# Second attention's planes reloaded one by one, the third plane copied on the chip, keys and the first quarter of queries ahead of the rest

## The reference, cut to what matters

```python
# layer 0: wavelet bands of x; ll is [8,128,32,32], N = 1024
q, k, v = conv1x1(ll, qkv_w)                 # 8 heads of 16 channels
attn = clip(l2norm(q) @ l2norm(k).T * 16**-0.5)
attn = softmax(keep the 512 largest of each row)
ll_out = group_norm(conv1x1(attn @ v, proj_w))
high_out = high + alpha * gn(conv1x1(silu(gn(dwconv3x3(high)))))
out = x + 0.1 * iwt(ll + ll_out, high_out)
out = out + 0.1 * gn(conv1x1(gelu(gn(conv1x1(out, w1))), w2))
# layer 1: one head of 16 channels over n = 4096 pixels
q, k, v = Wq x + bq, Wk x + bk, Wv x + bv
attn = softmax(q.T k / 4)                    # [4096, 4096]
x = gamma * (Wo (v attn.T) + bo) + x
```

## Time and profile before

| what | value |
|---|---|
| median of three runs | 5599.7 us |
| the profiled execution's own time | 5598.09 us |
| its span | 5596.3 us |
| PE, PE weight load, DVE, ACT, POOL busy | 85%, 55%, 83%, 76%, 5% |
| line 565 (PE): busy, idle just before it | 848.3 us, 115.2 us |
| line 1940 (DVE): busy, idle just before it | 1396.5 us, 291.9 us |
| mean granted clock of TensorE | 0.916 of full speed |

### The profile page before, as it was taken

How to read it: one execution, slowest core, us unless ns; L and a number is a source line. 1 busy time by engine, 2 the same in 40 slices (tenths; PEclk the granted TensorE clock), 3 DMA queues, 4 the chain that set the end, 5 groups by cost and what they waited for, 6 DMA issues and landing times.

```text
span 5596.3 us, 93339 instructions
## 1 busy us (share of the span) xinstructions
PE 4769.4 (85%) x30180; PEld 3089.7 (55%) x30180; DVE 4622.6 (83%) x9087; ACT 4266.1 (76%) x6779; POOL 261.7 (5%) x125
## 2 busy tenths in 40 slices
PE   4444899988999889988999889998899979997799
PEld 2001366654666446663666546664566636664588
DVE  4888799987999789987999879997899979996553
ACT  3884799948998589966999489985899669995333
POOL 2001000020000200010000200002000100000000
PEclk7555899998999989998999989999899989999899
DMA  1001200012001110012000120011200120001100
GB/s 57 7 11 51 63 15 16 15 57 66 16 20 49 38 48 18 16 61 63 15 16 14 58 66 16 20 44 37 54 16 18 60 64 15 16 13 44 36 12 16
DMA packets 101990, 187.43 MB, mean 33 GB/s; under 512 B 47640, under 2 KB 52664, under 8 KB 95832
## 3 DMA queue, kind: packets, MB, share of 16 engines
q1 hardware_dynamic: 101464, 181.02, 11.2%
HBM read 110.09 MB, written 69.47 MB: 32 GB/s over the span
## 4 chain that ended last, share of the span: by engine, by line
DVE 37%; PE 32%; issue 16%; ACT 7%; DMA 3%; SPq 2%; DVEq 1%; POOL 1%; ACTq 0%; POOLq 0%
PE PS L599 11%; DVE M L1772 8%; DVE MX L1940 8%; PE PS L565 5%; DVE work L1763 5%; PE PS L541 3%; ACT work L1194 3%; DVE work L1755 3%; DVE arena L1869 3%; PE PS L583 3%; PE PS L531 2%; PE PS L463 2%; ACT work L1247 1%; PE PS L1068 1%; PE PS L978 1%
## 5 line engine op out<-in xcount | busy, mean ns | idle before, releaser
L599 PEld LDWEIGHTS PS<-V,work 128*128 128x128 f32 x16384 | 2102.7, 192 | 163.4 <-ACT work L1255 23.0
L599 PE MATMUL PS<-V,work 128*128 128x129 f32 x16384 | 2122.1, 276 | 13.6 <-ACT work L1255 12.3
L1194 ACT ACTIVATE work<-arena,T 128x1024 bf16<-128x1024 f32 x1504 | 1715.5, 1144 | 63.0 <-DVE T L1713 47.8
L1940 DVE TENSOR_REDUCE MX<-PS 128x1 f32<-128x512 f32 x2048 | 1396.5, 686 | 291.9 <-PE PS L565 276.5
L1255 ACT ACTIVATE work<-PS 128x1024 f32<-128x1024 f32 x1024 | 1042.2, 1019 | 314.0 <-PE PS L583 312.1
L565 PE MATMUL PS<-KP,QP 96*128 96x512 bf16 x2048 | 848.3, 416 | 115.2 <-DMA QP<-scr 57.6
L1772 DVE MAX8 M<-work 128x8 f32<-128x512 f32 x1024 | 651.8, 681 | 0.5
L1186 ACT ACTIVATE arena<-PS 128x1024 f32<-128x1024 f32 x512 | 524.3, 1024 | 151.8 <-PE PS L463 142.6
L583 PE MATMUL PS<-QP,KP 99*128 99x512 bf16 x2048 | 620.5, 385 | 22.7 <-ACT work L1255 19.4
L1869 DVE SCALAR_TENSOR_TENSOR arena<-PS,work 128x512 f32<-128x512 f32 x896 | 601.3, 684 | 28.7 <-ACT work L1247 18.4
L1247 ACT ACTIVATE work<-PS 128x512 f32<-128x512 f32 x896 | 514.8, 592 | 112.9 <-PE PS L531 109.6
(11 more groups left out here) (193 smaller groups left out, 4158.2 us busy)
## 6 DMA issues: line engine op xcount, KB each, us to landing
work<-scr SPq DMA_DIRECT2D x752, 32.0 KB, 1.8
work<-in_x SPq DMA_DIRECT2D x16, 1024.0 KB, 6.7
arena<-in_x SPq DMA_DIRECT2D x8, 2048.0 KB, 10.8
scrX<-arena SPq DMA_DIRECT2D x8, 2048.0 KB, 6.7
XR<-scrX SPq DMA_DIRECT2D x64, 256.0 KB, 2.7
out<-YO SPq DMA_DIRECT2D x64, 256.0 KB, 2.1
scr<-work SPq DMA_DIRECT2D x24, 512.0 KB, 2.6
scrL<-work SPq DMA_DIRECT2D x24, 512.0 KB, 8.0
```

The lines of the kernel that those rows point to most:

```text
L599: last = mm(PS[:, 5 + i // 2, 136 * (i % 2):136 * (i % 2) + 129], P1[:, (16 * j + k) % 3, t, 128 * i:128 * i + 128], V1[:, mt, :], start=( ...
L1194: A(junk[:, m % 2, :], scores(h, i), ACT.Sign, scale=-1.0, bias=T[:, h % 2, i:i + 1], accum_out=CA[:, h % 2, i:i + 1]).then_inc(s["ca"], 1)
L1940: V.reduce_max(MX[:, c % 2, i, w:w + 1], PS[:, maxbank(c, k, l0), :], AX.X).then_inc(s["mr"], 1)
```

## The change

Three things change, all of them in DMAs, on SP's list.

First, the operands of the second attention. Plane 2 is no longer stored and reloaded: each 16-row block of plane 2 is copied from PT1 to its place by four copies of 16 rows by 2 KB (32 KB), one for each quarter of the pixels. Planes 0 and 1 are still stored by four DMAs each, but the loads of a plane wait for that plane alone (scrw1 for plane 0, scry1 for plane 1). The keys come first, over all pixels (three loads of plane 0, two of plane 1), then the first quarter of the queries (five loads of 32 KB), then, behind a wait for p12, the four key copies and one query copy of plane 2. These fifteen raise qp1, and the first maximum waits for them alone. The other three quarters of the queries follow (five loads of 96 KB, three copies of 32 KB) and raise a new semaphore qp2, for which the first maximum of chunk 2 waits.

Second, head 0 of the next image. The store of plane 0 is followed by its six loads, then come the stores of planes 1 and 2, the two on-chip copies of plane 2, and the four loads of plane 1, each group behind a semaphore of its own (scrw, scrv, scru).

Third, three guards on ACT: before its first eviction of head 1 (which writes over PT1) it also waits for qp1 and qp2, and before the first exponential of a chunk 0 (which writes over PT) for scru.

```diff
@@ -281,15 +281,26 @@
                         if t in parts:
                             sp.dma_start(QK0[HD * j:HD * j + HD, h % 3, w, :], scr0[t, d, w, :]).then_inc(done, 16)
 
-            def load_planes(parts):
-                for w, dst in ((1, KP1), (0, QP1)):
-                    for j, pair in enumerate(TERMS):
-                        if pair[w] in parts:
-                            sp.dma_start(dst[HD * j:HD * j + HD], scr1[pair[w], HD * w:HD * w + HD, :]).then_inc(s["qp1"], 16)
-
-            def store_plane(n, t, made):
+            def store_plane1(f, t, made, done):
+                sp.wait_ge(s[made], f + 1)
+                for j in range(4):
+                    sp.dma_start(scr1[t][:, N0 * j:N0 * j + N0], PT1[32 * j:32 * j + 32, t, :]).then_inc(s[done], 16)
+
+            def load_plane1(w, dst, t, cols, done):
+                for j, pair in enumerate(TERMS):
+                    if pair[w] == t:
+                        sp.dma_start(dst[HD * j:HD * j + HD, cols], scr1[t, HD * w:HD * w + HD, cols]).then_inc(s[done], 16)
+
+            def copy_plane1(w, dst, t, parts, done):
+                for j, pair in enumerate(TERMS):
+                    if pair[w] == t:
+                        for i in parts:
+                            sp.dma_start(dst[HD * j:HD * j + HD, N0 * i:N0 * i + N0],
+                                         PT1[32 * i + HD * w:32 * i + HD * w + HD, t, :]).then_inc(s[done], 16)
+
+            def store_plane(n, t, made, done):
                 sp.wait_ge(s[made], (n + 1) * 2)
-                sp.dma_start(scr0[t].rearrange("p w n -> p (w n)"), PT[:, t, :]).then_inc(s["scrw"], 16)
+                sp.dma_start(scr0[t].rearrange("p w n -> p (w n)"), PT[:, t, :]).then_inc(s[done], 16)
 
             def head0_late():
                 for j, pair in enumerate(TERMS):
@@ -404,25 +415,34 @@
                 if fin:
                     load_done(f, False)
                 if opn:
-                    store_plane(n, 0, "p0")
-                    store_plane(n, 1, "p1")
+                    store_plane(n, 0, "p0", "scrw")
                     sp.wait_ge(s["vt"], (n + 1) * 2)
                     sp.sem_inc(s["free"], 1)
-                    sp.wait_ge(s["scrw"], n * 48 + 32)
-                    load_head(0, (0, 1))
-                    store_plane(n, 2, "p2")
+                    sp.wait_ge(s["scrw"], (n + 1) * 16)
+                    load_head(0, (0,))
+                    store_plane(n, 1, "p1", "scrv")
+                    store_plane(n, 2, "p2", "scru")
                     head0_late()
+                    sp.wait_ge(s["scrv"], (n + 1) * 16)
+                    load_head(0, (1,))
                 if fin:
-                    for a, made in enumerate(("p10", "p11", "p12")):
-                        sp.wait_ge(s[made], f + 1)
-                        for j in range(4):
-                            sp.dma_start(scr1[a][:, N0 * j:N0 * j + N0], PT1[32 * j:32 * j + 32, a, :])                                .then_inc(s["scrw1" if a < 2 else "scry1"], 16)
-                    sp.wait_ge(s["scrw1"], (f + 1) * 128)
-                    load_planes((0, 1))
+                    store_plane1(f, 0, "p10", "scrw1")
+                    store_plane1(f, 1, "p11", "scry1")
+                    first, rest = slice(0, N0), slice(N0, N1)
+                    sp.wait_ge(s["scrw1"], (f + 1) * 64)
+                    load_plane1(1, KP1, 0, slice(0, N1), "qp1")
                     sp.wait_ge(s["scry1"], (f + 1) * 64)
-                    load_planes((2,))
+                    load_plane1(1, KP1, 1, slice(0, N1), "qp1")
+                    load_plane1(0, QP1, 0, first, "qp1")
+                    load_plane1(0, QP1, 1, first, "qp1")
+                    sp.wait_ge(s["p12"], f + 1)
+                    copy_plane1(1, KP1, 2, range(4), "qp1")
+                    copy_plane1(0, QP1, 2, range(1), "qp1")
+                    load_plane1(0, QP1, 0, rest, "qp2")
+                    load_plane1(0, QP1, 1, rest, "qp2")
+                    copy_plane1(0, QP1, 2, range(1, 4), "qp2")
                 if opn:
-                    sp.wait_ge(s["scrw"], (n + 1) * 48)
+                    sp.wait_ge(s["scru"], (n + 1) * 16)
                     for h in range(1, 3):
                         load_head(h)
                 if fin:
@@ -555,8 +575,10 @@
                     if c == 0 and k == 1 and l0:
                         pe.wait_ge(s["de"], (b + 1) * 6)
                     if k == 0 and c == 0:
-                        pe.wait_ge(s["qp1"], b * 192)
+                        pe.wait_ge(s["qp1"], b * 240)
                         pe.wait_ge(s["v1c"], b * 8)
+                    if k == 0 and c == 2:
+                        pe.wait_ge(s["qp2"], b * 128)
                     if k == 0 and c >= 2:
                         pe.wait_ge(s["y1"], a * NCH + c + (1 if l0 else 0))
                     elif k == 0 and c == 1:
@@ -1209,8 +1231,10 @@
                     if h >= 2:
                         act.wait_ge(s["pv"], (b * NH + h - 2) * NT + i + 1)
                     if h == 1 and i == 0:
-                        need(act, s["scrw1"], b * 128)
+                        need(act, s["scrw1"], b * 64)
                         need(act, s["scry1"], b * 64)
+                        need(act, s["qp1"], b * 240)
+                        need(act, s["qp2"], b * 128)
                         need(act, s["xs"], b * 16)
                     act.wait_ge(s["S"], (b * NH + h) * NT + i + 1)
                     stored(h, i)
@@ -1251,6 +1275,8 @@
                         return
                     act.wait_ge(s["st1"], a * 128 + j * 16 + k + 1)
                     act.wait_ge(s["pv1"], a * 128 + j * 16 + (k + 1 if j or k else 3))
+                    if l0 and j == 0 and k == 0:
+                        need(act, s["scru"], (b + 1) * 16)
                     u = pairbanks(k, l0)
                     A(P1[:, (16 * j + k) % 3, :, :].rearrange("p t n -> p (t n)"), PS[:, u:u + 2, :].rearrange("p a n -> p (a n)"),
                       ACT.Exp, scale=0.25).then_inc(s["e1"], 1)
```

More of the change, by code:

```diff
@@ L257, in dwt_attention_kernel @@
           st e p pv o od rd odr ol oc pj fnd fsum dll cv pw x1 dgl f1 hc ge f2 f2c f2n x2 xs q1 q1c p10 r11 p11 p12
-          scrw1 scry1 qp1 v1p v1c m mr mp mt mpt mq st1 e1 pv1 on nt xr0 xr1 y1 out0 out1 dset dimg dpr pimg g1 g2 g3 g4
+          scrv scru scrw1 scry1 qp1 qp2 v1p v1c m mr mp mt mpt mq st1 e1 pv1 on nt xr0 xr1 y1 out0 out1 dset dimg dpr pimg g1 g2 g3 g4
           g5 gs u1 u2 u3 u4 u5 hs qn ye si de dn bc bw xg xl sth eh ph dld dls kon dc1 dc2 free""".split()
```

## The result

| what | before | after |
|---|---|---|
| median of five runs | 5599.06 us | 5550.86 us |
| lowest to highest | 5597.75 to 5604.44 | 5544.52 to 5553.66 |
| the profiled execution's own time, its span | 5598.09, 5596.3 | 5553.66, 5551.9 |

The ratio is 0.9911, 95% interval 0.9898 to 0.9925: faster by 48.2 us, where 52.4 us were forecast. The profiled execution is the slowest of the five of after, so the spans differ by 44.4 us only.

A forecast was written before the change was run, and what follows sets the result against it. The prediction took the first maximum's wait for a DMA into QP1, 57.6 us over eight times, as the bound. Gains of 39.5 + 6.8 + 6.1 = 52.4 us gave 5547 us, range 5539 to 5555.

The forecast's parts named there:

- The gate, full transitions: Seven full transitions: the first maximum waits 0.75 us for ACT's last value copy instead of the DMA; gain 39.5 us.
- The steps inside it: SP's queue after plane 0 is ready: queries issued by 8.8 us, plane 2 copies by 11.8, landed at 13.9.
- The last transition: At the last first maximum the DMAs stay the later half, landing 13.9 us after plane 0 is ready; gain 6.8 us.
- Head 0: Next image's head 0: its scores' wait for on-chip copies goes, moving ACT's whole chain forward; gain 6.1 us.
- the full shift: Behind the first maximum nothing is deducted from the gain, with up to 3 us for a transition as the bound.
- two margins: Behind the first maximum: ACT needs 18.1 us against DVE's 18.2; scrL's stores land about 1 us before `apart` needs them.
- scrL's margin: scrL's stores come forward to 674.3 us, `apart`'s waiting second instruction to 675.5; margin about 1 us.
- the case of early values: Clock in the value stage: all last value copies come 1.5 us earlier; 5536 us, chance 12%.
- That rival: scrL's stores: `apart` waits 1 to 3 us in each full transition, 14 us given back; 5561 us, chance 14%.
- ACT's chain "just fits": Behind the first maximum ACT's bands and counts need 18.1 us, DVE's third threshold comes at 18.2.
- The rule weighed against the trace: Skill page's batching advice, about 2.0 us fixed per DMA: fifteen pieces one after another cost 30 us; trace rows show overlap.
- Pieces in series: Rival at the first maximum's loads: each piece lands before the next moves, 18 us lost eight times; 5740 us, chance 3%.

The follow-up runs named there:

- experiment 5: The whole change with its five 128 KB key loads each cut into four of 32 KB, same bytes; 5595.29 us, ratio 0.9992 to the kernel before.
- experiment 2: The kernel before with only head 0's DMAs reordered as in the change, second attention's DMAs as before; 5597.77 us, ratio 0.9999.
- experiment 4: The whole change, but the first maximum waits for all queries (qp2 as well); 5561.63 us, ratio 0.9935 to the kernel before.
- experiment 7: The whole change with head 2's loads put behind the scrX and scrL stores in SP's list; 5550.97 us, ratio 0.9909 to the kernel before.
- experiment 6: The whole change, but the wait for ACT's last value copy moved from the first maximum to V1's first use; 5552.93 us, ratio 0.9915.
- experiment 1: The second attention's part of the change alone, head 0's DMAs in their old order; 5552.84 us, ratio 0.9916 to the kernel before.
- experiments 3 to 6: The third is the whole change with plane 2 stored and reloaded through DRAM, 5554.10 us, ratio 0.9918; the others have their own lines.

## Why the prediction was right, and where its terms were off

*The gate, full transitions (39.5 us).* V to S gave 39.2 us, and the gate became ACT's value copy in all seven, with 0.14 us behind the copy and an idle of 0.78 us before PE's first maximum where 0.75 was taken. The steps inside it held to 0.1 us in the queue. What made them hold was SP's list: experiment 5 doubles the pieces of the gate (thirty for fifteen) at equal bytes and loses everything.

*The last transition (6.8 us).* 7.0 us; the data came at P + 13.75, forecast P + 13.9. The last gate copy was issued at P + 11.25 (forecast P + 11.2) and landed 2.4 us later (forecast 2.5 to 2.7). The first of the five copies took 3.8 us: it was issued at P + 8.8, while loads were still under way (the last of the query loads landed at P + 12.3), and landed at P + 12.55. Only the last copy counts, and by then the loads were through. So the median of line 298 of after (over its key and query copies) would have been the wrong row to add:

```profile
L298 SPq DMA_DIRECT2D KP<-arena x32: 512/589/819, 650.2 to 5168.9; - x32
...
DMA to landing us min/median/max: 2.0/3.2/4.2
```

*Head 0 (6.1 us).* The step held as far as it went: Q to P fell by 6.9 us and the wait for `work<-work` is gone. The step that failed is the last of it, that this moves ACT's whole chain and so the end. The change is 2.0 us faster than the gate alone, which tells little, and head 0 alone takes the time of before (ratio 0.9999, 5 us to either side), where 6.1 us were forecast. Where it is lost stays open: in the profile of experiment 2 it comes back between the gate and the next Q, in that of experiment 4 it does not. Without this term the forecast would have been 46.3 us less than before; 48.2 were measured, and the interval (42 to 57 us) holds both sums, so the total can't judge the term.

*Where gains could be given back.* I took the full shift and named two margins. scrL's margin of 1 us was too large by 1.7: the stores land at P + 38.7 to 39.3 and `apart`'s second instruction waits in four transitions. They are the four in which V came at P + 16.5; with V at P + 17.4 or later there is no wait. So the case of early values, priced as a gain by itself, brings this wait with it. (The 6.9 us by which `apart` was to come forward are 6.5 by the prediction's own terms, 39.5 + 6.1 over seven.) One of them, the second:

```profile
1328.56 0.74 DVE L1781 TENSOR_SCALAR work<-arena,T 128x1024 f32<-128x1024 f32 x1
1329.93 0.75 DVE L1781 TENSOR_SCALAR work<-arena,T 128x1024 f32<-128x1024 f32 x1 [0.63 <-DMA scrL<-work]
```

That rival was right in kind and small in size: 2.7 us in all, and without it (experiment 7) the median is the same. ACT's chain "just fits" was right as well, 18.2 against 18.1 us; its price showed only when the gate was opened earlier still (experiment 6).

*What I did not price* is the 6.1 us more from S to the next Q. It goes with the clock. Windows of the first transition, of before from 3 us behind S on, of after from S on (us, busy of PE, PEld, DVE, ACT, POOL, PEclk, DMA share, GB/s):

```profile
663.30:698.30 35.00, 25.54 (x53) 6.26 (x53) 31.83 (x60) 25.54 (x44) 0.00 (x0) 0.50 0.27 110
698.30:703.30 5.00, 4.83 (x34) 3.61 (x33) 4.73 (x8) 5.00 (x10) 0.00 (x0) 0.96 0.01 2
```

```profile
659.00:661.00 2.00, 1.22 (x4) 0.34 (x4) 1.59 (x3) 2.00 (x4) 0.00 (x0) 1.00 0.12 21
661.00:697.00 36.00, 26.23 (x54) 6.50 (x54) 32.60 (x62) 32.23 (x54) 0.00 (x0) 0.50 0.33 122
697.00:702.00 5.00, 5.00 (x20) 3.71 (x19) 3.47 (x6) 4.83 (x9) 0.00 (x0) 0.50 0.01 2
```

Before, the granted clock was back at 2.4 GHz 38 us behind S and PE did 34 matmuls in the next 5 us. After, the low stretch (0.50, 1.2 GHz) began 2 us behind S and not ahead of it, and PE was still in it 38 to 43 us behind S while it had work without a break: 20 matmuls in 5 us. This is so in three transitions of after; in the other four the low stretch ended some 40 us behind S. The trace's clock records have 52 us at the low level from S to the next Q in most transitions of before, 54.6 us in the first five of after; over all seven it is 380 against 392 us. In experiment 1 the first three transitions have 44 to 48 us, and there S to the next Q takes 622 to 624 us against 625 to 627. The correlation is shown, though not without exceptions (the fifth of experiment 1 takes 628.9 us with 51 at the low level); that an earlier gate must lengthen the low stretch is not, since experiment 1 opens it as early. What sets the phase stays open. The 3.2 us less from P to V were luck of the same kind: 47 us at the low level there before, 38 after.

*The rule weighed against the trace.* Pieces in series would have made 5740 us; experiment 5 with thirty pieces ahead of the gate took 5595. The Trainium skill, page "DMA: Bandwidth & Descriptors", section "Anatomy of one DMA", gives about 2.0 us fixed for each DMA. That section is on DMAs issued by GpSimd, while all of this kernel's are SP's, and it lays most of the 2 us to the receipt of the last byte; that they are paid one after another is a reading of the prediction and of experiment 5's rival, and the page does not say it. The trace fits a latency of that order (the plane stores landed 1.6 to 1.7 us after issue, loads of 32 to 128 KB 2.8 to 5.3 us), and it is not paid one after another. That page's advice to batch, section "Bandwidth", still points the right way here, for another reason than its descriptors: the queue that issues them.

## What to carry to other kernels

Where a wait for data ends a stage, write down for each piece when it is ready, when the issuing queue reaches it and when it is wanted; put first what the first instruction needs, and count the queue's 0.4 to 0.6 us for each DMA as the price of cutting. Then look for who becomes late next, and on how many engines at once: here two chains ended together, and relieving either alone gave nothing that could be measured, both together 19 us, a part of which goes with the clock. A shift counts only as far as it reaches the end: head 0's 6.9 us were plain in the trace and not to be found in the time.

## What the runs showed of the hardware beyond that

- The same instructions up to the first Q took 636.3, 631.7, 632.0, 631.6 and 630.1 us in five profiles (the change and experiments 3 to 6, whose lists are alike up to there). A spread of 6 us from nothing in the program is as large as the term that I was after, so one profile against another can't show head 0's worth; only the means of several runs can.
- P to V takes 16.55 us in transitions whose value matmuls ran at 2.4 GHz and up to 20.4 us where the low stretch fell on them. Where it falls moves a transition by 3.9 us, and it falls on other transitions in each kernel's profile (most of all on the fourth and sixth in after, on the second in before).
- A copy from SBUF to SBUF costs 0.59 us in SP's queue against 0.42 us for a load from DRAM of the same size (medians of lines 298 and 292 of after).
